# Attention in a fused two-layer kernel: row maxima spread over the partitions by two transfers through memory instead of by TensorE, and the work between the score blocks put in another order

## The chip, the cores and the metric

The kernel runs on one core of one Trainium2 chip, as one launch. Its time is the device time of that launch in microseconds (us). Three runs of the kernel before took 1915.51, 1917.42 and 1915.51 us (median 1915.51). The change is judged against that median.

## The reference

Two layers over `x` of shape (4, 1024, 128). Only the attention of layer 0 is touched by the change:

```python
# layer 0: xn = layernorm(x)
qkv = xn @ W_qkv                       # 128 -> 3 * 64 * 16, 16 heads of 64
scores = einsum('bqhd,bkhd->bhqk', q, k) / 8
weights = softmax(scores)              # row maximum, exp, sum, division
s = einsum('bhqk,bkhd->bqhd', weights, v).reshape(b, s, 1024) @ W_out
x = x + s * silu(experts(xn) + shared_expert(xn))   # 8 experts, top 2
# layer 1: a recurrence over time and a gated MLP with 4-bit weights and inputs
```

W_qkv is large (scaled by 8), so scores are large and the row maximum has to be taken off before the exponential.

## The kernel before, in words

The program has stages in a row: norm and router, attention (`layer0_attention`), expert tiles, layer 1. Attention takes the stretch from about 75 to 1507 us of the span.

Attention works on pairs of heads: 4 batches times 8 pairs are N = 32 pairs, and one pair of heads is 16 steps. In step `t` the scores of 128 keys (`kt = t % 8`) against 512 queries (`hf = t // 8`, the half) are computed for both heads at once: a block of 128 partitions (keys) by 2 x 512 columns (queries). Keys lie on the partitions, so the maximum over keys for each query can't be read off this block. It is found beforehand from a rougher product with queries on the partitions:

- `row_max` on TensorE multiplies q_hi by k_hi (two matmuls of 64 x 128 x 512) into the one PSUM tile `ps_m`; VectorE reduces it (L1546). Eight such steps make a "unit", the maxima of 512 queries; the last reduction (L1549) leaves them in `mxw`, 128 partitions x 2 heads x 4 groups of queries.
- These maxima have to lie along the columns, the same on every partition. Before the change TensorE does this: `max_rows` (L1241) transposes `mxw` by a product with the identity, VectorE multiplies by a mask (`shifts`, L1560) into `shift`, `spread` (L1293) multiplies ones by `shift` into a score bank, and ScalarE copies the result to SBUF (`keep_shift`, L1444, the tile `shift_all`, which is named `qkv_raw` in the trace because it lies over it).
- For each step ScalarE then writes the negated maxima into the score bank (`seed`, L1449), TensorE adds the scores in three products of high and low parts (`scores`, L1286), and ScalarE takes the exponential (L1464) into a ring of eight `probs` tiles.

TensorE multiplies V by `probs` into `ps_v` (`values`, L1301), two steps later. GpSimd adds the `probs` tiles up (L1529), and the denominators come from a product of ones with that sum.

Two steps are a "visit"; a pair has visits 0 to 7. In each visit TensorE does, in this order: `row_max`, `scores`, `scores`, `row_max`, then the first item of the table `VISIT`, then `values` for two steps, then the other items of `VISIT`. Items are: projections of K and Q for the next pair (K0, K1, Q0, Q1, halves of 512 tokens, L1214), rows of V (V0, V1, L1231), denominators (den0, den1, L1250), output projections (out0, out1, L1259), and max0, max1 (L1241). All items share one PSUM bank, `ps_x`, so each waits until the one before it has been read. Of a K or Q projection ScalarE reads the high part (L1412), then VectorE the rest (`low`, L1554).

The two score banks `ps_s` alternate, and `seed` of step t+2 waits for the exponential of step t. The order of every engine is fixed by this hand-written table and by the code; nothing is rearranged at run time. SyncE issues the transfers in program order and stops at each wait. In the trace k_hi, k_lo, q_hi, q_lo of even pairs are called `e_ew`, and den, rden, raw, attn are `e_y_row`, because later tiles lie over them.

Of the kernel before, what the change touches and what calls it, by code (L numbers as in the profile page):

```python
# [75 lines left out]
def layer0_norm_and_router(nc, ctx, g):  # L76
# [61 lines left out]
    with nc.Block() as block:  # L138
        @block.sync
        def _(sp):  # L140
# [24 lines left out]
        def _(pool):  # L165
# [27 lines left out]
        def _(act):  # L193
# [794 lines left out]
def layer0_attention(nc, ctx, g):  # L988
# [9 lines left out]
    EARLY = 3  # L998
# [3 lines left out]
    PRESETS = 5  # L1002
    LATE_PRESETS = 7
# [1493 lines left out]
```

## Time and profile before

| what | value |
|---|---|
| median of 3 runs | 1915.51 us |
| the profiled execution, its device time | 1918.03 us |
| its span in the trace | 1916.2 us |
| time outside the span | 1.8 us |
| granted TensorE clock, whole span | 0.982 |
| attention stage | about 75 to 1507 us, 32 pairs |

All durations below come from the profiled execution, which is 2.5 us above the median of the runs. Its page gives the busy time of each engine: TensorE 93%, VectorE 78%, ScalarE 78%, GpSimd 75% of the span. In the attention stage the engines work beside each other in the same 16-step rhythm, so a share of the whole span does not say which one sets the pace there; that is read from the order in time within one pair, where an engine without idle time before its instructions is the one that the others wait for.

### The profile page before, as it was taken

Reading aid. Unit: us, or ns where it says so; the run is one execution under the profiler, and the core shown is the slowest. Engines: PE = TensorE matmul, PEld = TensorE weight load, DVE = VectorE, ACT = ScalarE, POOL = GpSimd, SP = SyncE. Lnnn points to the kernel's source line nnn. Section 1 sums busy time; section 2 is a strip of 40 time slices with the busy share of each in tenths; the row PEclk is TensorE's granted clock in tenths of the full one; section 3 lists DMA queues with packets and bytes.
Section 4 is the critical chain, followed back from the end, with each engine's and each line's share of the span. In section 5 each row is a group of like instructions: output and inputs, shape, how many; then the busy total and the mean of one; then the engine's idle time right before and its main releaser. Section 6 shows DMA issues by size and latency. Waiting matters only on the chain. (4 is left out here: it accounts for less than half of the span.)

```text
span 1916.2 us, 32241 instructions
## 1 busy us (share of the span) xinstructions
PE 1776.4 (93%) x9630; PEld 958.1 (50%) x9630; DVE 1486.4 (78%) x2052; ACT 1485.6 (78%) x2017; POOL 1434.9 (75%) x870
## 2 busy tenths in 40 slices
PE   5799999999999999999999999999999899985688
PEld 4444444444444444444444444444444488863456
DVE  6777777777777777777777777777777698888896
ACT  4488888888888888888888888888888688874553
POOL 4388888888888888888888888888888456765663
PEclk9999999999999999999999999999999999997898
DMA  7101010101011010101010101011010477531000
GB/s 248 46 13 55 11 56 15 59 11 55 22 44 42 25 55 11 55 11 55 12 55 19 55 20 46 22 44 56 11 55 11 153 230 247 158 99 50 1 17 28
DMA packets 98438, 108.95 MB, mean 57 GB/s; under 512 B 8161, under 2 KB 88097, under 8 KB 95202
## 3 DMA queue, kind: packets, MB, share of 16 engines
q1 hardware_dynamic: 93410, 98.26, 16.1%
q0 software_dynamic: 4992, 10.27, 1.6%
q8 instruction: 16, 0.26, 0.1%
q14 instruction: 20, 0.16, 0.0%
HBM read 53.12 MB, written 27.38 MB: 42 GB/s over the span
## 5 line engine op out<-in xcount | busy, mean ns | idle before, releaser
L1529 POOL TENSOR_TENSOR psum_k<-psum_k,probs 128x1024 f32<-128x1024 f32 x384 | 926.4, 2412 | 183.7 <-ACT probs L1464 168.6
L1546 DVE TENSOR_REDUCE mxh<-ps_m 128x2 f32<-128x1024 f32 x518 | 628.4, 1213 | 276.1 <-PE ps_m L1273 275.7
L1464 ACT ACTIVATE probs<-ps_s 128x1024 f32<-128x1024 f32 x512 | 496.4, 1022 | 132.4 <-PE ps_s L1286 93.2
L1301 PE MATMUL ps_v<-probs,V 128*64 128x512 f32 x2056 | 489.8, 597 | 0.0
L1449 ACT ACTIVATE ps_s<-qkv_raw 128x1024 f32<-128x1024 f32 x449 | 445.9, 1030 | 7.1
L1570 DVE RECIPROCAL e_y_row<-e_y_row 128x128 f32<-128x128 f32 x256 | 241.8, 945 | 30.2 <-ACT e_y_row L1420 21.1
L1301 PEld LDWEIGHTS ps_v<-probs,V 128*64 128x64 f32 x2056 | 137.6, 137 | 224.9 <-issue 188.4
L1529 POOL TENSOR_TENSOR psum_k<-probs 128x1024 f32<-128x1024 f32 x64 | 152.4, 2381 | 65.7 <-ACT probs L1464 57.9
L1286 PE MATMUL ps_s<-e_ew 64*128 64x512 f32 x1536 | 198.9, 390 | 1.1 <-ACT qkv_raw L1444 1.0
L1286 PEld LDWEIGHTS ps_s<-e_ew 64*128 64x128 f32 x1536 | 145.9, 184 | 28.6 <-ACT qkv_raw L1444 1.4
L859 POOL DMA_INDIRECT results<-e_y_row,e_y_at x92 | 103.7, 1128 | 67.4 <-ACT e_y_row L800 45.2
L1273 PE MATMUL ps_m<-e_ew 64*128 64x512 f32 x524 | 131.5, 498 | 11.4 <-DVE mxh L1546 10.2
L1273 PE MATMUL ps_m<-k_hi,q_hi 64*128 64x512 f32 x512 | 128.0, 496 | 4.0 <-DVE mxh L1546 3.6
L1273 PEld LDWEIGHTS ps_m<-e_ew 64*128 64x128 f32 x524 | 49.1, 184 | 114.8 <-DVE mxh L1546 68.2
L1286 PE MATMUL ps_s<-q_hi,k_lo 64*128 64x512 f32 x512 | 101.6, 391 | 0.0
L1286 PE MATMUL ps_s<-q_hi,k_hi 64*128 64x512 f32 x512 | 101.5, 391 | 0.0
L1286 PE MATMUL ps_s<-q_lo,k_hi 64*128 64x512 f32 x512 | 101.2, 389 | 0.0
L1273 PEld LDWEIGHTS ps_m<-k_hi,q_hi 64*128 64x128 f32 x512 | 47.6, 183 | 106.5 <-DVE mxh L1546 60.1
L784 ACT ACTIVATE e_relu<-e_ps_z 128x512 f32<-128x512 f32 x124 | 74.2, 598 | 26.5 <-PE e_ps_z L713 25.6
L905 DVE TENSOR_TENSOR e_h_lo<-e_relu,e_h_hi 128x512 fp32r<-128x512 f32 x124 | 87.5, 711 | 1.2 <-ACT e_h_hi L789 1.2
L901 DVE TENSOR_TENSOR e_relu<-e_relu 128x512 f32<-128x512 f32 x108 | 74.5, 690 | 15.5 <-ACT e_relu L784 15.2
L789 ACT ACTIVATE e_h_hi<-e_relu 128x512 fp32r<-128x512 f32 x124 | 78.2, 631 | 6.0 <-DVE e_relu L901 5.9
(322 smaller groups left out, 2938.1 us busy)
## 6 DMA issues: line engine op xcount, KB each, us to landing
e_ew<-w_split SPq DMA_DIRECT2D x23, 1024.0 KB
V<-e_x_raw SPq DMA_DIRECT2D x33, 512.0 KB, 3.6
xs_hi<-xh SPq DMA_DIRECT2D x16, 512.0 KB, 4.1
xs_lo<-xl SPq DMA_DIRECT2D x16, 512.0 KB, 4.7
rows<-in_blank_d SPq DMA_DIRECT2D x4, 1483.5 KB, 16.2
e_x_raw<-rows SPq DMA_DIRECT2D x23, 258.0 KB, 3.0
we_raw<-in_experts_d SPq DMA_DIRECT2D x33, 128.0 KB, 2.5
w_split<-we_hi SPq DMA_DIRECT2D x32, 128.0 KB, 1.9
```

The source lines that it names most:

```text
L789: nc.scalar.activation(h_hi[:, q % NH, :], r2[:, q % NH, :], ACT.Copy).then_inc(hi_done, 1)
L859: nc.gpsimd.indirect_dma_start(g.results[:, :], bass.IndirectOffsetOnAxis(ap=y_at[s][:, t, 0:1], axis=0), y_row[s][:, t, :], None).then_in ...
L901: nc.vector.tensor_tensor(r2[:, q % NH, :], r[:, q % NZ, :], r[:, q % NZ, :], ALU.mult).then_inc(sq_done, 1)
L905: nc.vector.tensor_tensor(h_lo[:, q % NH, :], r2[:, q % NH, :], h_hi[:, q % NH, :].bitcast(F32), ALU.subtract).then_inc(lo_done, 1)
L1273: ins = nc.tensor.matmul(m[:, x, :], q_hi[par][rows, q:q + P], k_hi[par][rows, kh * CH:(kh + 1) * CH], start=True, stop=True)
L1286: ins = nc.tensor.matmul(o[:, x, :], lhs[par][rows, keys], rhs[par][rows, qs], start=False, stop=True, skip_group_check=True)
L1301: ins = nc.tensor.matmul(ps_v[rows, :], V[par][:, kt, rows], probs[:, t % RING, x, :], start=kt == 0, stop=kt == KT - 1)
L1449: nc.scalar.activation(ps_s[t % 2][:, :, :], shift_all[:, :, :], ACT.Copy).then_inc(seeded, 1)
L1464: nc.scalar.activation(probs[:, t % RING, :, :], ps_s[t % 2][:, :, :], ACT.Exp, scale=SCALE).then_inc(p_done, 1)
L1529: nc.gpsimd.tensor_tensor(acc, probs[:, (t - 1) % RING, :, :] if kt == 1 else acc, probs[:, t % RING, :, :], ALU.add).then_inc(add_done, 1)
L1546: nc.vector.tensor_reduce(mxh[:, kh, t, :], max_bank(unit, i)[:, :, :], AX.X, ALU.max).then_inc(m_done, 1)
L1570: ins = nc.vector.reciprocal(rden[:, cols], den[:, cols])
```

## The change

TensorE no longer turns and spreads the maxima. The last reduction of a unit writes `mx` (128 x 2 x 4). SyncE waits for it and writes its 1024 values to memory (`peaks`, each 4 bytes at its own place), waits until they have landed, and reads them back into all 128 partitions (`peak[hf]`, 128 x 1024, 512 KB). Every seed, the first of a half too, is a copy of `peak[hf]` times -1; those of steps 3 and 15 (`BY_V`) are made by VectorE, the other 14 of a pair by ScalarE. The maxima run one more step ahead of the scores (`EARLY` 4 instead of 3).

The items stand in another order: at most one item stands before `values`, and den1, den0 are the last of their visits. K0 of a pair is computed in visit 7 of the pair two before it, not in visit 0 of the one before it. ScalarE's rounding of the next weights (`w_hi`) moves from visit 7 to visit 5, GpSimd's (`w_lo`) from the end of the pair to step 11, and the expert part from visit 4 to visit 0.

```diff
-    EARLY = 3
+    EARLY = 4
-    VISIT = [("out0", "K0"), ("den1", "Q0"), ("max1", "V0"), ("K1",), ("out1",), ("den0", "Q1"), ("max0", "V1"), ()]
-    LATE = ("K1", "out1")
+    VISIT = [("out0",), ("Q0", "den1"), ("V0",), ("K1",), ("Q1", "den0"), ("V1",), ("out1",), ("K0",)]
-    FIRST = ["K0", "Q0", "K1", "Q1", "V0", "V1", "V2", "max0", "V3"]
+    FIRST = ["K0", "Q0", "K1", "Q1", "V0", "V1", "V2", "V3", "K0+"]
+    BY_V = (3, 15)
...
+            def spread(unit, hf):          # on SyncE
+                sp.wait_ge(mx_done, unit + 1)
+                sp.dma_start(g.peaks[hf:hf + 1, :].rearrange("a (x t q) -> q (a x) t", x=2, t=4), mx[:, :, :],
+                             allow_slow_non_contiguous=True).then_inc(mx_out, 16)
+                sp.wait_ge(mx_out, unit * 16 + 16)
+                sp.dma_start(peak[hf][:, :, :].rearrange("p x c -> p (x c)"), g.peaks[hf:hf + 1, :].to_broadcast([P, 2 * CH])).then_inc(peak_in, 16)
             load_part(0)
+            spread(0, 0)
...
                 sp.dma_start(xs_lo[:, :].bitcast(F32), g.xl[:, batch].bitcast(F32)).then_inc(xs_in, 16)
+                spread(n * 2 + 1, 1)
                 expert_part(n)
                 load_part(n + 1)
+                spread(n * 2 + 2, 0)
+                spread(n * 2 + 3, 1)
                 expert_part(n + 1)
                 load_part((n + 2) % N)
+                spread(n * 2 + 4, 0)
                 sp.wait_ge(xa_done, reads(n + 1, "V1"))
                 move(0)
...
                     scores(n, par, t)
                     row_max(n * 2 + unit, i, other, unit % 2)
-                    if t % KT == KT - 1:
-                        pe.wait_ge(shift_done, n * 2 + t // KT + 2)
-                        pe.wait_ge(p_done, P0 + n * STEPS + t)
-                        spread(1 - t // KT, 0).then_inc(spread_ready, 1)
                     for name in VISIT[p][:1]:
-                        if name not in LATE:
-                            item(n, par, name, b)
+                        item(n, par, name, b)
...
-            def keep_shift(k):
-                act.wait_ge(spread_ready, k)
-                nc.scalar.activation(shift_all[:, :, :], ps_s[0][:, :, :], ACT.Copy).then_inc(seeded, 1)
+            def seed(n, t):                # on ScalarE
+                hf = t // KT % 2
+                if t % KT < 2:
+                    act.wait_ge(peak_in, peaks_of(n, t))
+                act.wait_ge(p_done, P0 + n * STEPS + t - 1)
+                nc.scalar.activation(ps_s[t % 2][:, :, :], peak[hf][:, :, :], ACT.Copy, scale=-1.0).then_inc(seeded, 1)
...
+            def seed(n, t):                # on VectorE, steps 3 and 15
+                v.wait_ge(p_done, P0 + n * STEPS + t - 1)
+                v.wait_ge(peak_in, peaks_of(n, t))
+                nc.vector.tensor_scalar(ps_s[t % 2][:, :, :], peak[t // KT][:, :, :], -1.0, None, ALU.mult).then_inc(seeded_v, 1)
...
-                shifts(n, "max1")
...
+                add_out(n, "out1")
+                seed(n, 15)
                 step(14)
```

TensorE, the end of visit 3 of an even pair, before (rows from the second `row_max`, named L1273, to the next visit's first; `shift1` holds the maxima of the second half):

```order
L1273 MATMUL ps_m<-k_hi1,q_hi1 128x512 x2
L1373 REGISTER_ALU
L1293 MATMUL ps_s0<-shift1,ones_r 128x512 x2
L1301 MATMUL ps_v<-probs,V0 64x512 x4
L1214 ISA
L1214 MATMUL ps_x<-xh,w_hi 128x512
L1215 REGISTER_ALU
L1215 MATMUL ps_x<-xl,w_hi 128x512
L1216 MATMUL ps_x<-xh,w_lo 128x512
L1270 REGISTER_ALU
L1273 MATMUL ps_m<-k_hi1,q_hi1 128x512 x2
```

The same place now (L1286 is `row_max` here, L1233 to L1235 the projection K1, L1311 `values`):

```order
L1286 MATMUL ps_m<-k_hi1,q_hi1 128x512 x2
L1233 ISA
L1233 MATMUL ps_x<-xh,w_hi 128x512
L1234 REGISTER_ALU
L1234 MATMUL ps_x<-xl,w_hi 128x512
L1235 MATMUL ps_x<-xh,w_lo 128x512
L1309 REGISTER_ALU
L1311 MATMUL ps_v<-probs,V0 64x512 x2
L1309 REGISTER_ALU
L1311 MATMUL ps_v<-probs,V0 64x512 x2
L1283 REGISTER_ALU
L1286 MATMUL ps_m<-k_hi1,q_hi1 128x512 x2
```

The spreading product L1293 is gone, and K1 stands ahead of `values` instead of behind it.

ScalarE at the same boundary, before (L1464 exponentials, L1444 the kept copy, L1449 the seed, L1412 the read of K1):

```order
L1464 ACTIVATE probs<-ps_s0 128x1024
L1464 ACTIVATE probs<-ps_s1 128x1024
L1444 ACTIVATE qkv_raw<-ps_s0 128x1024
L1449 ACTIVATE ps_s1<-qkv_raw 128x1024
L1412 ACTIVATE k_hi1<-ps_x 128x512
L1464 ACTIVATE probs<-ps_s0 128x1024
```

Now (L1472 exponentials, L1419 the read of K1, L1456 the seeds):

```order
L1472 ACTIVATE probs<-ps_s0 128x1024
L1472 ACTIVATE probs<-ps_s1 128x1024
L1419 ACTIVATE k_hi1<-ps_x 128x512
L1456 ACTIVATE ps_s0<-peak1 128x1024
L1456 ACTIVATE ps_s1<-peak1 128x1024
L1472 ACTIVATE probs<-ps_s0 128x1024
```

The read of K1 stands between the exponentials and the seeds, and the first seed of the half comes from `peak1`, which a transfer fills.

SyncE now, in an even pair (L1153 moves V, L1169 writes the maxima, L1172 reads them back):

```order
L1153 DMA V<-e_x_raw 128x8x128
L1183 ISA
L1183 DMA xs_hi<-xh 128x1024
L1184 REGISTER_ALU
L1184 DMA xs_lo<-xl 128x1024
L1168 REGISTER_ALU
L1169 DMA peaks<-mx 128x8x1
L1171 ISA
L1172 DMA peak<-peaks 128x1024
```

Before, the transfers of the expert part followed directly on `xs_lo`.

## Rows read from the trace of the kernel before

**Rows 1.** The page, its head and part 1.
```profile
span 1916.2 us, 32241 instructions
PE 1776.4 (93%) x9630; PEld 958.1 (50%) x9630; DVE 1486.4 (78%) x2052; ACT 1485.6 (78%) x2017; POOL 1434.9 (75%) x870
```

**Rows 2.** Instructions of line 1444, one per half pair: durations, first and last start.
```profile
L1444 ACT ACTIVATE qkv_raw<-ps_s x65: 1023/1032/1032, 75.2 to 1507.4; 128x1024 f32<-128x1024 f32 x65
```

**Rows 3.** Windows, visits 1, 4, 5, 7, then all eight: PE, PEld, DVE, ACT, POOL, clock.
```profile
753.81:759.92 6.11, 5.94 (x32) 2.71 (x32) 4.00 (x4) 5.00 (x6) 5.43 (x4) 1.00 0.03 11
...
771.13:776.10 4.97, 4.97 (x30) 2.23 (x29) 3.55 (x4) 4.25 (x5) 3.39 (x2) 1.00 0.00 0
776.10:782.26 6.16, 5.94 (x33) 2.68 (x32) 5.19 (x5) 5.37 (x8) 5.29 (x4) 1.00 0.03 11
...
787.89:792.58 4.69, 4.62 (x27) 2.12 (x26) 4.11 (x5) 3.86 (x5) 3.92 (x2) 1.00 0.40 112
sum 44.74, PE 43.52 PEld 20.85 DVE 34.02 ACT 37.30 POOL 36.97; mean PE 5.44 PEld 2.61 DVE 4.25 ACT 4.66 POOL 4.62
```

**Rows 4.** Timeline of TensorE in that pair: start, length, line, [idle before <- releaser].
```profile
755.62 0.50 PE L1273 MATMUL ps_m<-k_hi,q_hi 64*128 64x512 f32 x2
756.30 1.08 PE L1250 MATMUL ps_x<-psum_k,ones 128*64 128x512 f32 x4 [0.17 <-DVE e_ew L1554]
...
761.74 0.50 PE L1273 MATMUL ps_m<-e_ew 64*128 64x512 f32 x2
762.56 0.44 PE L1241 MATMUL ps_x<-ident,mxw 128*64 128x128 f32 x4 [0.32 <-DVE e_ew L1554]
762.83 1.89 PE L1301 MATMUL ps_v<-probs,V 128*64 128x512 f32 x8
...
767.37 0.50 PE L1273 MATMUL ps_m<-e_ew 64*128 64x512 f32 x2
767.94 0.49 PE L1293 MATMUL ps_s<-shift,ones_r 64*128 64x512 f32 x2
768.37 1.94 PE L1301 MATMUL ps_v<-probs,V 128*64 128x512 f32 x8
...
772.95 0.49 PE L1273 MATMUL ps_m<-e_ew 64*128 64x512 f32 x2
773.37 1.94 PE L1301 MATMUL ps_v<-probs,V 128*64 128x512 f32 x8
...
778.21 0.50 PE L1273 MATMUL ps_m<-e_ew 64*128 64x512 f32 x2 [0.22 <-DVE mxh L1546]
```

**Rows 5.** Timeline of ScalarE in visit 1 of that pair.
```profile
755.12 1.94 ACT L1464 ACTIVATE probs<-ps_s 128x1024 f32<-128x1024 f32 x2 [0.61 <-PE ps_s L1286]
757.42 0.60 ACT L1420 ACTIVATE e_y_row<-ps_x 128x512 f32<-128x512 f32 x1 [0.36 <-PE ps_x L1250]
757.91 1.97 ACT L1449 ACTIVATE ps_s<-qkv_raw 128x1024 f32<-128x1024 f32 x2
```

**Rows 6.** The page, part 5: group, busy, mean ns, idle before.
```profile
L1546 DVE TENSOR_REDUCE mxh<-ps_m 128x2 f32<-128x1024 f32 x518 | 628.4, 1213 | 276.1 <-PE ps_m L1273 275.7
```

**Rows 7.** The page, part 6: issues, KB each, median us to landing.
```profile
V<-e_x_raw SPq DMA_DIRECT2D x33, 512.0 KB, 3.6
xs_lo<-xl SPq DMA_DIRECT2D x16, 512.0 KB, 4.7
w_split<-we_hi SPq DMA_DIRECT2D x32, 128.0 KB, 1.9
```

**Rows 8.** DMA view, 1519.8 to 1520.7 us: queue, packets, MB, engines' share.
```profile
q1 hardware_dynamic: 244, 0.00, 12.3%
```

**Rows 9.** Timeline, visit 0 of the even pair that begins at 703.03: SyncE.
```profile
709.67 1.07 SPq L1171 DMA_DIRECT2D xs_lo<-xl  x1
```

**Rows 10.** Timeline, the start of attention: last reduction of the first unit, first exponentials.
```profile
68.12 0.17 DVE L1549 TENSOR_REDUCE mxw<-mxh 128x8 f32<-128x16 f32 x1
...
77.43 1.98 ACT L1464 ACTIVATE probs<-ps_s 128x1024 f32<-128x1024 f32 x2
```

More of the change, by code:

```diff
@@ L1121, in rounded, with seeds_before, peaks_of @@
         upto = sum(k[0] in "KQ" for k in names[:names.index(name) + 1])
-        return upto if n is None else n * 4 + 4 + upto
+        return upto if n is None else n * 4 + 5 + upto
+    def seeds_before(t):
+        return t - sum(k < t for k in BY_V)
+    def peaks_of(n, t):
+        return n * 32 + (t // KT + 1) * 16
     def added(t):
@@ L1234, in v_rows @@
                 ins.then_inc(x_ready, 1)
-            def max_rows(n, name):
-                bank_free(n, name)
-                pe.wait_ge(mx_done, 1 if n is None else n * 2 + (2 if name == "max1" else 3))
-                for x, rows in enumerate(HEADS):
-                    ins = nc.tensor.matmul(bank(n, name)[rows, 0:P], mxw[:, x, :], g.ident[:, :], start=True, stop=True)
-                ins.then_inc(x_ready, 1)
             def denominators(n, name):
@@ L1288, in scores @@
                 ins.then_inc(s_ready, 1)
-            def spread(hf, k):
-                for x, rows in enumerate(HEADS):
-                    ins = nc.tensor.matmul(ps_s[k][:, x, :], ones_r[rows, :], shift[hf][rows, :], start=True, stop=True)
-                return ins
             def values(n, par, t, seen):
@@ L1339, in _ @@
             first_max(0, 4, 5, 6, 7)
-            first("V0", "V1", "V2", "max0")
+            first("V0", "V1", "V2", "V3")
             pe.wait_ge(hi_done, rounded(None, "Q1"))
             first_max(1, *range(EARLY))
-            first("V3")
+            pe.wait_ge(n_read, 1)
+            pe.wait_ge(m_done, KT + EARLY)
+            for k in range(2):
+                for x, rows in enumerate(HEADS):
+                    ins = nc.tensor.matmul(ps_s[k][:, x, :], k_hi[0][rows, 0:P], q_hi[0][rows, 0:CH], start=True, stop=True)
+            ins.then_inc(armed, 1)
+            first("K0+")
             pe.wait_ge(preset, LATE_PRESETS)
+            pe.wait_ge(xa_done, AHEAD["a"])
             pe.wait_ge(xv_done, AHEAD["v"])
-            pe.wait_ge(n_read, 1)
             for x, rows in enumerate(HEADS):
                 nc.tensor.matmul(ps_v[rows, :], ones[:, :], probs[:, 0, x, :], start=True, stop=False)
-            pe.wait_ge(shift_done, 1)
-            pe.wait_ge(m_done, KT + EARLY - 1)
-            spread(0, 1)
-            spread(0, 0).then_inc(spread_ready, 1)
             for n, par in pairs(pe):
-                b = (n + 1) // PAIRS % B
                 for t in range(STEPS):
                     p = t // 2
+                    b = (n + (2 if p == VISITS - 1 else 1)) // PAIRS % B
                     unit, i = maximum(t)
@@ L1689, in _ @@
                 add_out(n, "out0")
+                seed(n, 3)
                 step(2)
-                low(n, "K0", nxt)
                 step(3)
+                low(n, "Q0", nxt)
+                expert_part(n)
+                step(4)
                 inverse(n, 1, 0)
-                step(4)
-                low(n, "Q0", nxt)
                 step(5)
-                shifts(n, "max1")
                 inverse(n, 1, 1)
@@ L2450, in layouts @@
     blank[:, D] = 2 * NT + np.arange(ROUTED * CH)
-    mask = np.zeros((2, DH, 4), np.float32)
-    for j in range(4):
-        mask[:, j, j] = -1.0
     return {
```

153 lines of the change are left out of this document (73 added, 80 removed).

## The prediction, as it was put on record before the change was run

> **What bounds the kernel now.** I read the page first: TensorE is busy 93% of the span, VectorE, ScalarE and GpSimd 75 to 78% [rows 1]. That makes TensorE the suspect and nothing more. Line 1444 runs once per half pair, 65 times from 75.2 to 1507.4 us [rows 2], so a pair takes 2 x 1432.2 / 64 = 44.76 us, and attention is 32 of them, 1432 of 1916 us. Next come the windows, one per visit, of the pair that begins at 747.84: the eight add up to 44.74 us, in which TensorE is busy 43.52, ScalarE 37.30, GpSimd 36.97, VectorE 34.02, at a granted clock of 1.00 [rows 3]. Since the ends of matmuls are modelled, I then looked at starts in the timeline: nearly every TensorE instruction follows the one before it at a fixed distance, and the exceptions are few [rows 4]. ScalarE's exponentials wait for TensorE [rows 5], and VectorE's reductions waited 275.7 us for `ps_m` over the kernel [rows 6]. So TensorE sets the pace, and a pair is worth what is taken out of its row.
>
> **What goes out of TensorE's row.** A plain distance from the second `row_max` to what follows is 772.95 to 773.37, 0.42 us. Against it, per pair:
> - Spreading product: 767.37 to 768.37 is 1.00 us with L1293 between, so it costs 0.58, twice: 1.16.
> - max0 and max1: 761.74 to 762.83 is 1.09 us, so 0.67 each, of which 0.40 is the wait for VectorE's `low` (the bank must be read). Twice: 1.34.
> - den1 behind the second `row_max` waits for `low` of K0: 755.62 to 756.30, 0.68 instead of 0.42: 0.26 in visit 1. Now den1 stands behind Q0 and `values`.
> - Visit 5: the second `row_max` comes 778.21 - 776.10 = 2.11 us after the first, against 755.62 - 753.81 = 1.81 in visit 1, since out1's addition stands before the reduction on VectorE: 0.30. In the new table out1 is one of the items before `values`, done earlier.
>
> All from [rows 3, 4]. Sum 3.06 us a pair; 44.74 - 3.06 = 41.68. K0 only moves. In the new order a visit with one item should last 4.96 (visit 4 now: 4.97), and visits 1 and 4 with two items 5.86 (visit 5 now: 6.16 - 0.30) [rows 3]: 6 x 4.97 + 2 x 5.86 = 41.5, nearly the same.
>
> **Do the other engines keep up with 41.7?** ScalarE loses two of 16 copies of about 0.98 us (two take 1.97 [rows 5]): 37.30 - 1.97 = 35.3 busy. VectorE loses two products of 512 columns and gains two seeds of 1024 columns. The trace has no such instruction with SBUF in and PSUM out; the nearest is the reduction of 1024 columns out of PSUM, 1.21 us [rows 6]; below, it could be half of that, above, I allow 1.4. I take 1.2; VectorE then has about 35. GpSimd does the same 36.97. None reaches 41.7, but a visit can still be too long for one. The tightest is visit 6, with two reductions, a reciprocal, out1's addition and the seed of step 15. Visit 5 now has the same with the expert difference in the seed's place, 5.19 us busy [rows 3], against a visit of 4.97: about 0.1 to 0.3 late, caught up in visit 7. ScalarE reads the item between the exponentials and the seeds: exponentials begin 1.31 into a visit (755.12 - 753.81), are through 1.82 later, the projection ends about 3.2 into it, its read is followed by the seed after 0.49 (757.42 to 757.91), so seeds start at about 3.7 and the first is done at 4.7 [rows 5]; the next visit's scores begin at 4.97 + 0.33. Half a microsecond of slack. I put 0.10 us a pair for new small waits, with 0 and 0.6 as ends.
>
> **The transfers.** They leave no instruction on TensorE, but the first seeds of a half wait for them, and behind these on ScalarE stand all later ones. The last `row_max` of a unit is the second of visit 1 or 5: 1.81 + 0.50 + 1.21 + 0.17 [rows 3, 4, 6, 10], about 3.8 us into it (4.0 in visit 5, where a reciprocal stands before). The seeds that need it are due 3.7 into visit 3 or 7, and may be 0.5 late. That is free time of 5.86 + 4.97 + 3.7 - 3.8 + 0.5 = 11.2 us for the second half and 2 x 4.97 + 3.7 - 4.0 + 0.5 = 10.1 us for the first.
> What they take: the read back is 512 KB to 128 partitions like the move of V, 3.6 us; behind other traffic 4.7 [rows 7]. The write is 1024 pieces of 4 bytes, 64 for each of 16 DMA engines, and the trace has none like it. From below: a store of 128 pieces of 1 KB lands in 1.9 us; the move of V, also 1024 pieces though of 512 bytes, in 3.6 [rows 7]. On the rate of 4-byte pieces I found one stretch: 244 packets in 0.9 us, with the engines 12.3% busy [rows 8], so 0.123 x 16 x 900 / 244 = 7 ns of engine time each, but only one in 59 ns per engine (16 x 900 / 244). If 59 ns is the pace at which they are made, 64 need 3.8 us beside the 1.9: 5.7. I take 4.6, between 3.6 and 5.7, nearer neither; as an upper end 8 us, if a write to memory of 4 bytes costs twice such a read. The chain is 4.6 + 3.6 + 0.3 for SyncE's two waits = 8.5 us, with ends of 7.5 and about 12. Under 10.1 it costs nothing.
> In even pairs the write stands in the same queue behind `xs_lo`, issued 709.67 - 703.03 = 6.64 into visit 0 and landed 4.7 later, at 11.3 [rows 7, 9]; the maxima are ready at 4.97 + 3.8 = 8.8. So the chain begins up to 2.5 us late there, in the half that has 11.2: 8.5 + 1.0 to 2.5 is 9.5 to 11.0. Just free.
> On SyncE the blocking waits stand before the expert part, whose stores and loads have whole visits of time, and before the move of V, which is needed only in the next pair's visit 1, over 15 us later.
> The Trainium skill, "DMA: Bandwidth & Descriptors", section "Rules for kernel authors", says that a non-contiguous last dimension lowers to one descriptor per element, and its "Specifications" that under 512 bytes the DMA engine reads, modifies and writes. The first agrees with the 1024 pieces that I count; of the second no row of this trace shows a price for stores, and it speaks for the upper end above.
>
> **Start and end.** Before, 9.31 us lie between the first unit's maxima and the first exponentials (68.12 to 77.43) [rows 10]. Now the chain of 8.5, a seed of 1.0 and about 1.1 for scores give 10.6 or more: +2 us with the extra step and K0+. The end is unchanged.
>
> **Sum.** 32 x (3.06 - 0.10) - 2 = 93 us. The profiled execution took 1918.03 (span 1916.2 and 1.8 around it): 1825. It stands 2.5 above the median of the runs, so 1915.5 - 93 = 1822.5; I say 1822.
>
> **The rivals.**
> - A, the forecast: TensorE stays the pace, the chain is covered. 44.74 - 41.5 = 3.2 a pair and no start cost gives 1813; 0.6 of new waits and some more at the start 1838. Own range 1812 to 1842. Chance 0.72.
> - B, the chain is late in part: 10.1 to 12.2 us. At 11.2 the first half of each pair is 1.1 us late, the even pairs' second half about 1.5 (queueing), so 32 x 1.1 + 16 x 1.5 = 59 us given back: 1881; milder cases down to 1840. For it: 59 ns a piece and the queue behind `xs_lo`; against: 3.6 us for as many pieces of V. Chance 0.12.
> - C, slower: the store of 4-byte pieces is so slow that the seed of the first step of each half waits for it. Every us above 10.1 and 11.2 stops ScalarE and then TensorE; from (c - 10.1) + (c - 11.2) = 3.0, c = 12.2, nothing is gained, a bit sooner with the queue. At c = 14 it is 3.9 + 2.8 - 3.0 = 3.7 us a pair: 1915.5 + 118 = 2034. It needs a store of about 8.3 us or more, or a read back that is slowed since all partitions ask for the same 4 KB. Against it: 7 ns of engine time a piece. Chance 0.09. The read-modify-write rule of the Trainium skill named above would work in this direction.
> - D, VectorE or ScalarE takes over in visits 6 and 7 (a seed of 1.4, a read between exponentials and seeds that comes too late): 1 us a pair, 32 us: 1854. For it: 5.19 against 4.97; against: whole-pair sums of 35 against 41.7. Chance 0.07.
>
> **How the numbers follow.** The median of three runs can tell 0.2% (4 us) from nothing. A, D and most of B are faster: 0.72 + 0.07 + 0.09; within 0.2%: 0.02, from B; slower: C and the rest of B, 0.10. The range takes A, D and half of B: 1810 to 1870, 0.85.
>
> **What would show it.** Right: pairs of 41.6 to 42 us; no matmul between the second `row_max` and the item; the second `row_max` 1.81 after the first in every visit; ScalarE's seeds of steps 0, 1, 8, 9 issued at once behind the item's read; the maxima's write landing in 4 to 6 us, the read back in 3.6 to 4. Wrong: idle time of ScalarE before those seeds, released by the read back (B, C); distances of 2.1 and more between the two `row_max` of visit 7 (D); a store above 8 us. A TensorE clock below 1.00 in the stretch would be something I have not reckoned with.

## The result, and the profile after

The changed kernel takes 2200.75 us (median of 4 runs, 2195.82 to 2212.92); beside them the kernel before took 1916.47 us (1915.51 to 1919.24). The ratio is 1.149, with a 95% interval of 1.144 to 1.154: slower by 15%. The forecast was 1822 us with a range up to 1870, and the sign was wrong too.

The head of the page after and its part 1, against [rows 1]:

```profile
span 2195.8 us, 32039 instructions
PE 1860.2 (85%) x9247; PEld 996.3 (45%) x9247; DVE 1519.2 (69%) x2053; ACT 1433.5 (65%) x1954; POOL 1438.9 (66%) x868
```

Every engine's share has fallen, TensorE's from 93 to 85% and ScalarE's from 78 to 65%. No engine took over, so all of them wait for something else. Part 5 (busy, mean ns | idle before, releaser) and part 6 (KB each, us to landing) name it; the V row answers to that of [rows 7]:

```profile
L1456 ACT ACTIVATE ps_s<-qkv_raw 128x1024 f32<-128x1024 f32 x224 | 221.7, 1021 | 141.2 <-DMA qkv_raw<-peaks 141.2
L1456 ACT ACTIVATE ps_s<-peak 128x1024 f32<-128x1024 f32 x224 | 222.2, 1023 | 129.5 <-DMA peak<-peaks 129.5
...
qkv_raw<-peaks SPq DMA_DIRECT2D x33, 512.0 KB, 4.2
V<-e_x_raw SPq DMA_DIRECT2D x33, 512.0 KB, 5.1
peak<-peaks SPq DMA_DIRECT2D x32, 512.0 KB, 4.4
```

ScalarE's seeds wait 270.7 us for the read back of the maxima, in 64 halves: 4.23 us each. The read back itself lands in 4.2 to 4.4 us (3.6 reckoned). The rest is the store, seen in SyncE's timeline (start, length, line) and in its row of the waits (in all, times, longest):

```profile
807.40 0.39 SPq L1169 DMA_DIRECT2D peaks<-mx  x1
817.71 0.32 SPq L1172 DMA_DIRECT2D qkv_raw<-peaks  x1
...
SPq L1172 <- DMA peaks<-mx: 610.3, 64, 11.6
```

From the store's issue to the read back's issue 10.3 us pass here and 10.0 in the mean of all halves; SyncE waits 9.5 of them for the store, where 4.6 were forecast. The same boundary on ScalarE and on TensorE:

```profile
814.68 1.94 ACT L1472 ACTIVATE probs<-ps_s 128x1024 f32<-128x1024 f32 x2 [2.11 <-PE ps_s L1302]
816.67 0.60 ACT L1419 ACTIVATE k_hi<-ps_x 128x512 fp32r<-128x512 f32 x1
822.07 1.97 ACT L1456 ACTIVATE ps_s<-qkv_raw 128x1024 f32<-128x1024 f32 x2 [4.80 <-DMA qkv_raw<-peaks]
```

```profile
818.43 0.50 PE L1286 MATMUL ps_m<-e_ew 64*128 64x512 f32 x2
823.15 2.71 PE L1302 MATMUL ps_s<-e_ew 64*128 64x512 f32 x12 [4.22 <-ACT ps_s L1456]
825.66 0.63 PE L1286 MATMUL ps_m<-e_ew 64*128 64x512 f32 x2
```

The seeds could have begun at 817.27 (822.07 - 4.80). They begin 14.7 us after the store's issue, so the free time was 9.9 us and the chain 14.7, against 10.1 and 8.5 forecast. This is a first half; of the second half that follows, the store on SyncE and the seeds on ScalarE:

```profile
833.15 0.38 SPq L1169 DMA_DIRECT2D peaks<-mx  x1
```

```profile
848.39 1.97 ACT L1456 ACTIVATE ps_s<-peak 128x1024 f32<-128x1024 f32 x2 [4.41 <-DMA peak<-peaks]
```

Here 10.8 us were free (11.2 forecast) and the chain took 15.2. And the scores behind the first of these stalls last 2.71 us where they last 1.55 elsewhere. The windows (length, busy of PE, PEld, DVE, ACT, POOL, granted clock, DMA share, GB/s) say why:

```profile
819.00:823.00 4.00, 0.00 (x0) 0.00 (x0) 1.32 (x2) 0.93 (x1) 2.97 (x4) 1.00 0.84 244
823.00:826.00 3.00, 2.85 (x14) 1.92 (x14) 0.00 (x0) 2.39 (x5) 0.00 (x0) 0.57 0.00 1
826.00:829.00 3.00, 3.00 (x14) 0.85 (x12) 2.35 (x3) 1.85 (x2) 1.99 (x1) 0.86 0.00 0
829.00:832.00 3.00, 3.00 (x20) 1.89 (x19) 2.32 (x3) 2.34 (x4) 1.60 (x3) 1.00 0.46 127
...
829.24:835.11 5.87, 5.87 (x34) 2.68 (x32) 4.39 (x6) 5.29 (x7) 4.39 (x4) 1.00 0.78 260
835.11:840.13 5.02, 5.02 (x32) 2.67 (x30) 4.01 (x4) 4.16 (x6) 4.01 (x3) 1.00 0.15 24
```

TensorE stands still for 4 us, and in the 3 us behind that its granted clock is 0.57, near the lower of its two levels (1.2 instead of 2.4 GHz). The last two rows are visits away from the stall, against [rows 3]: 5.87 and 5.02 us, where 5.86 and 4.96 were forecast. Between the stalls the new order does what it was reckoned to do.

A pair lasts 53.23 us: the 512 exponentials start between 83.8 and 1783.9, so 16 steps take 16 x 1700.1 / 511.

### The profile page after: what moved, and what is told of

Same layout as the page of the kernel before. It is cut to its first block and busy times, and to the rows that moved or that the text cites. A ratio compares the mean times of both kernels' runs of the same rounds, so it can differ in the third digit from the quotient of the medians.

```text
span 2195.8 us, 32039 instructions
## 1 busy us (share of the span) xinstructions
PE 1860.2 (85%) x9247; PEld 996.3 (45%) x9247; DVE 1519.2 (69%) x2053; ACT 1433.5 (65%) x1954; POOL 1438.9 (66%) x868
## 5 line engine op out<-in xcount | busy, mean ns | idle before, releaser
L1472 ACT ACTIVATE probs<-ps_s 128x1024 f32<-128x1024 f32 x512 | 503.6, 1023 | 189.6 <-PE ps_s L1302 188.9
L1311 PE MATMUL ps_v<-probs,V 128*64 128x512 f32 x2056 | 505.9, 613 | 0.0
L1302 PE MATMUL ps_s<-e_ew 64*128 64x512 f32 x1536 | 236.8, 445 | 125.9 <-ACT ps_s L1456 123.6
L1456 ACT ACTIVATE ps_s<-qkv_raw 128x1024 f32<-128x1024 f32 x224 | 221.7, 1021 | 141.2 <-DMA qkv_raw<-peaks 141.2
L1456 ACT ACTIVATE ps_s<-peak 128x1024 f32<-128x1024 f32 x224 | 222.2, 1023 | 129.5 <-DMA peak<-peaks 129.5
L1311 PEld LDWEIGHTS ps_v<-probs,V 128*64 128x64 f32 x2056 | 136.1, 143 | 268.3 <-issue 246.6
L1302 PEld LDWEIGHTS ps_s<-e_ew 64*128 64x128 f32 x1536 | 159.6, 210 | 170.9 <-ACT ps_s L1456 138.1
L1302 PE MATMUL ps_s<-q_hi,k_hi 64*128 64x512 f32 x512 | 121.0, 467 | 104.9 <-ACT ps_s L1456 104.9
L1286 PE MATMUL ps_m<-e_ew 64*128 64x512 f32 x524 | 135.6, 514 | 7.0 <-DVE mxh L1550 6.3
L1286 PE MATMUL ps_m<-k_hi,q_hi 64*128 64x512 f32 x512 | 132.0, 512 | 0.0
L1286 PEld LDWEIGHTS ps_m<-e_ew 64*128 64x128 f32 x524 | 53.7, 202 | 152.5 <-issue 108.1
L1286 PEld LDWEIGHTS ps_m<-k_hi,q_hi 64*128 64x128 f32 x512 | 52.3, 201 | 141.9 <-issue 103.8
L1302 PE MATMUL ps_s<-q_lo,k_hi 64*128 64x512 f32 x512 | 116.0, 445 | 0.0
L1302 PE MATMUL ps_s<-q_hi,k_lo 64*128 64x512 f32 x512 | 116.0, 446 | 0.0
L1302 PEld LDWEIGHTS ps_s<-q_hi,k_hi 64*128 64x128 f32 x512 | 55.8, 214 | 122.8 <-ACT ps_s L1456 116.0
L1272 PE MATMUL ps_x<-e_y_row,wo 128*64 128x512 f32 x260 | 91.2, 788 | 0.8 <-issue 0.8
```

What stands on the lines that cost most here:

```text
L1272: ins = nc.tensor.matmul(ps_x[rows, :], wo[1 - par][:, rows], attn[:, :], start=True, stop=True)
L1286: ins = nc.tensor.matmul(m[:, x, :], q_hi[par][rows, q:q + P], k_hi[par][rows, kh * CH:(kh + 1) * CH], start=True, stop=True)
L1302: ins = nc.tensor.matmul(o[:, x, :], lhs[par][rows, keys], rhs[par][rows, qs], start=False, stop=True, skip_group_check=True)
L1311: ins = nc.tensor.matmul(ps_v[rows, :], V[par][:, kt, rows], probs[:, t % RING, x, :], start=kt == 0, stop=kt == KT - 1)
L1456: nc.scalar.activation(ps_s[t % 2][:, :, :], peak[hf][:, :, :], ACT.Copy, scale=-1.0).then_inc(seeded, 1)
L1472: nc.scalar.activation(probs[:, t % RING, :, :], ps_s[t % 2][:, :, :], ACT.Exp, scale=SCALE).then_inc(p_done, 1)
```

## The experiments

The names in the diffs are those of the changed kernel unless said otherwise. Kernels of one group ran beside each other, each with runs of the kernel before: 1916.6 us in the first group, 1925.5 in the second, 1925.7 in the third.

**Smaller cost of the store, no transfers at all, and a real alternative.** First, pieces of 32 bytes:

```diff
-sp.dma_start(g.peaks[hf:hf + 1, :].rearrange("a (x t q) -> q (a x) t", x=2, t=4), mx[:, :, :], ...
+sp.dma_start(g.peaks[hf:hf + 1, :].rearrange("a (q x t) -> q (a x) t", x=2, t=4), mx[:, :, :], ...
```

> The changed kernel with one difference in place: each partition writes its 8 maxima side by side (32 bytes, 128 pieces) instead of at 1024 places of 4 bytes. The maxima then come back in another order, so the values are wrong, and the exponential has a scale of 1/8000 instead of 1/8 so that all stays finite; the work is the same. Theory T1, the store of 4-byte pieces is the whole miss: the wait for the store falls from about 10 us to about 2 to 2.5, the read back stays at 4.3, the chain is 6.5 to 7.5 and under the 9.9 that are free; ScalarE's waits for the read back (270.7 us in the changed kernel) go to under 10, the granted clock goes back to 1.00, and the time is 1815 to 1835. Theory T2, the read back and the queueing matter as much as the store (the 512 KB read from one 4 KB row, transfers ahead in the queue): the waits fall only by half, 1950 to 2050. Theory T3, the new order itself runs slower than reckoned: above 1850 although ScalarE waits for no transfer.

Measured: 1839.01 us, ratio 0.959 (0.958 to 0.961). SyncE waits 86.4 us over 65 times for the store, 1.3 each, and no seed waits for a transfer. Second, the store and the read back happen once, ahead of the loop:

```diff
 with sp.Fori(0, N // 2) as i:
-    spread(n * 2 + 1, 1)
-    spread(n * 2 + 2, 0)
...
```

> The changed kernel with the two transfers done only once, at the start; all seeds of all pairs use the first unit's maxima, so no seed in the loop waits for a transfer, and 64 writes and read backs are gone. The values are wrong, with the exponential's scale at 1/8000 so that all stays finite. T1 and T2: this is the ceiling of the new order, pairs of 41.7 us, 1815 to 1830. T3: above 1850. The difference to the run with packed writes is what the transfers cost beside the stall (contention, clock): T1 says under 10 us.

Measured: 1840.51 us (0.960, 0.959 to 0.962), the same as with 32-byte pieces. So transfers that are in time cost nothing, and some 1838 us, not 1822, is what the new order is worth. Both times lie above the ranges of T1 (up to 1835 and 1830) and below the 1850 of T3: T1 has the cause, but its ranges were built around the prediction's 1822, which leaves out small waits and a later start (see below). Third, VectorE turns the maxima in blocks of 32x32, and four stores write 8 rows of 128 bytes each:

```diff
+nc.vector.transpose(mxT[:, :], mx[:, :]).then_inc(mx_done, 1)
...
+for k in range(4):
+    q = slice(k * 32, (k + 1) * 32)
+    sp.dma_start(g.peaks[hf:hf + 1, :].rearrange("a (c q) -> (a c) q", c=8)[:, q], mxT[k * 32:k * 32 + 8, :]).then_inc(mx_out, 16)
```

> The changed kernel, all values right, but VectorE turns the 128 x 8 maxima in blocks of 32 x 32 first, and SyncE writes them with four transfers of 8 rows of 128 bytes each (32 pieces in all) instead of 1024 pieces of 4 bytes. T1: four issues of about 0.4 us and 2 us to land, so 3.5 to 4 us for the store, chain 8 to 8.5 us with the turn, under 9.9 for the first half and under 11.2 for the second but for even pairs behind xs_lo, where it is near the edge: 1815 to 1850. T2: 1900 and more. T3: above 1850 without waits for a transfer.

Measured: 1837.27 us, 0.959 (0.958 to 0.961). It beats both kernels. SyncE's timeline, and the windows of visits 0, 1, 3 of the pair from 714.30 and the sum of its eight:

```profile
723.50 1.34 SPq L1173 DMA_DIRECT2D peaks<-mxT  x4
725.71 0.34 SPq L1176 DMA_DIRECT2D peak<-peaks  x1
```

```profile
714.30:719.42 5.12, 5.03 (x30) 2.19 (x28) 4.51 (x5) 3.79 (x5) 4.79 (x6) 1.00 0.00 0
719.42:725.30 5.88, 5.88 (x34) 2.69 (x33) 4.42 (x7) 5.30 (x7) 5.41 (x4) 1.00 0.04 12
...
730.43:735.45 5.02, 5.02 (x29) 2.39 (x27) 3.85 (x4) 4.40 (x6) 4.66 (x3) 1.00 0.00 0
...
sum 42.25, PE 42.09 PEld 19.90 DVE 35.88 ACT 35.14 POOL 37.30; mean PE 5.26 PEld 2.49 DVE 4.48 ACT 4.39 POOL 4.66
```

Four stores take 2.2 us together, TensorE is busy 42.09 of 42.25 us, and the chain is 2.2 + 3.9 to 4.1 + 0.2 = 6.3 to 6.5 us under a free time of 10. Behind `xs_lo`, in the second half of even pairs, the four stores take 3.3 us in the mean, still in time.

**Which stores are slow?** Small stores to memory were added to the kernel before, on SyncE's queue where it is idle, one behind the other, 16 times over the kernel, whose time they leave at 1920 to 1929 us. Their form is

```diff
+def probe(n, k, dst, src):
+    sp.dma_start(dst, src, allow_slow_non_contiguous=True).then_inc(pr_sem, 16)
+    sp.wait_ge(pr_sem, n * 64 + (k + 1) * 16)
```

> The kernel before, with six small transfers once per two pairs on SyncE's queue, one after the other with nothing else in flight, and nobody waiting for their data. Kernel time about that of before (1916, up to +5). Prices, T1: 1024 stores of 4 bytes as in the change 9 to 10 us; 128 stores of 32 bytes 2 us; 512 stores of 4 bytes 5 to 6; 8 rows of 512 bytes 2; 1024 stores of 4 bytes that lie 64 bytes apart: 9 to 10 if the number of pieces is the price, much less if it is that neighbouring pieces share a line of memory; 1024 loads of 4 bytes: 4 to 6 if writing to memory is the dear part, 9 to 10 if the pace of pieces is. T2: the 1024 stores take under 6 us when nothing is ahead of them in the queue.

> The kernel before with eight small stores to memory per two pairs, one behind the other, on a queue that is idle there, each with a wait for its completion: first 1,024 pieces of 4 bytes, 64 bytes apart; second 8 rows of 512 bytes; third 1,024 pieces of 4 bytes side by side (the changed kernel's); fourth 128 pieces of 4 bytes side by side; fifth 128 pieces 64 bytes apart; sixth 1,024 pieces 512 bytes apart; seventh 1,024 pieces 32 bytes apart; eighth the 8 rows again. Theory line (pieces in the same 64 bytes wait for each other): the third and the fourth take 8 to 9 us, the first, fifth and sixth 2.2 to 3 us, the seventh (two to 64 bytes) in between or like the first. Theory small write (any write to memory of 4 bytes is slow, for it has to be read, merged and written): all but the second and the eighth take 6 to 9 us. Theory count: the first, third, sixth and seventh take 8 us, the fourth and fifth 2 to 3 us; the 512 pieces that took as long as 1,024 speak against it already.

> The kernel before with small stores one behind the other on the idle queue: 128 pieces of 4 bytes at a spacing of 32, 16, 8 and 4 bytes (2, 4, 8 and 16 of them in the same 64 bytes), then 16 pieces of 4 bytes side by side (one stretch of 64 bytes), 128 pieces of 8 bytes side by side (8 to 64 bytes), 128 of 16 bytes (4 to 64 bytes), and 8 rows of 512 bytes. Theory turns (each further piece in the same 64 bytes costs some 0.4 us): 2.9, 3.7, 5.3 and 8.4 us; the 16 pieces 8.4 as well; 8 bytes 5.3, 16 bytes 3.7. Rival threshold (only full chains of 4-byte neighbours are slow, or pieces below some size): the first three 2.5 us, or all of them 8 us; the pieces of 8 and 16 bytes 2.5 us. The kernel with pieces of 16 bytes, whose store took 2.2 us in the mean instead of 3.5 to 4, speaks against the same price for pieces of 16 bytes.

> The kernel before with small stores on the idle queue, all of 4-byte pieces: 16, 32, 64, 128 and 256 side by side, then 32 at a spacing of 8 bytes, 16 at a spacing of 64 bytes, and 8 rows of 512 bytes. The run before showed 1.3 us (median) for 16 pieces side by side and 8 us for 128, with the same 16 pieces in each 64 bytes, and 1.4, 1.9, 3.5 and 8.0 us for 128 pieces 32, 16, 8 and 4 bytes apart. Theory chain (a DMA is dealt out to 16 engines in order, so of n pieces each engine has n/16 neighbours, and those that it writes into the same 32 bytes go one behind the other, at about 1 us each): 16, 32, 64, 128, 256 side by side take 1.4, 1.9, 3.5, 8 and 8 us, since the chain is 1, 2, 4, 8 and 8 long; the 32 pieces 8 bytes apart 1.9. Theory place (only the pieces per 64 bytes count, and 16 alone are an exception of one stretch): 32, 64, 128 and 256 all 8 us; the 32 pieces 8 bytes apart 3.5.

One pass of the second of these, in SyncE's timeline (each start less the one before is a store with its wait):

```profile
740.80 0.38 SPq L1167 DMA_DIRECT2D pr_out<-pr  x1
743.40 0.29 SPq L1167 DMA_DIRECT2D pr_out<-pr8r  x1
744.63 0.39 SPq L1167 DMA_DIRECT2D pr_out<-pr  x1
753.15 0.33 SPq L1167 DMA_DIRECT2D pr_out<-pr  x1
761.51 0.33 SPq L1167 DMA_DIRECT2D pr_out<-pr  x1
764.07 0.37 SPq L1167 DMA_DIRECT2D pr_out<-pr  x1
```

1,024 pieces of 4 bytes take 2.60 us when they are 64 bytes apart and 8.52 when they are neighbours; 128 neighbours take 8.36, and 2.56 when apart. Issue to next issue, mean in us over the 16 passes of one run each:

| stores of 4-byte pieces | us |
|---|---|
| 1,024: side by side | 9.4, 9.6 |
| 1,024: 32, 64, 512 bytes apart | 2.8, 2.4, 2.5 |
| 512 side by side | 9.1 |
| 256 side by side | 8.1 |
| 128: side by side | 7.7, 8.0, 8.0 |
| 128: 8, 16, 32, 64 bytes apart | 3.5, 1.9, 1.4, 2.0 |
| 64, 32, 16 side by side | 6.8, 3.1, 1.3 |
| 16 side by side, in the third experiment | 1.8 (1.3 to 3.3) |
| 32, 8 bytes apart | 3.1 |
| 16, 64 bytes apart | 1.3 |
| 128 of 8, 16, 32 bytes, side by side | 3.4, 2.1, 1.6 |
| for comparison, a load of the 1,024 | 2.3 |

"Count" is wrong from 128 upward, and "any 4-byte write" is wrong: what is slow are small pieces next to each other, 32 or more of them. With 128 pieces the price fades at a spacing of 16 bytes; with 32 pieces a spacing of 8 bytes took off nothing (3.1 us both times). My finer theories fell as well. That pieces in the same 64 bytes go one behind the other doesn't hold for 16 alone (1.3 us). The chain per DMA engine gave 1.9 and 3.5 us for 32 and 64 pieces; they took 3.1 and 6.8, and the rise ends at 128 where it should end. The trace doesn't show which engine writes which piece, so the mechanism stays open; the table is what is shown. It isn't the engines' work: in the DMA view of the changed kernel from 807.40 to 817.70, 40 slices (busy tenths), its 1,040 packets are through after six slices of 0.26 us, and what follows is waiting for completion.

```profile
DMA  0002770000000000000000000000000000000000
...
q1 hardware_dynamic: 1040, 0.00, 4.5%
```

The Trainium skill, "DMA: Bandwidth & Descriptors", section "Anatomy of one DMA — SWDGE (gpsimd) path", says that the semaphore's update waits until the last byte has landed, that this can take surprisingly long for a target in HBM, and that it is most of a fixed cost of about 2 us. The trace agrees in the order, packets first and then a wait, for a transfer that SyncE issued. The size roughly holds for pieces 64 bytes apart (2.4 us in all) and not for neighbours (9.4 to 9.6); here the measurement decides.

**Inside the kernel.** To the alternative (1837 us) a second store of the same maxima was added ahead of the read back, once as 1,024 neighbours, once 64 bytes apart:

```diff
+sp.dma_start(g.probe[0:1, 0:1024 * s].rearrange("a (c q s) -> q (a c) s", c=8, s=s)[:, :, 0:1], mx[:, 0:8].unsqueeze(2), ...)  # s = 1 or 16
+sp.wait_ge(mx_out, unit * 80 + 80)
```

> The kernel that turns the maxima on VectorE (1837 us), with one more store between its own store and the read back: the maxima once more as 1,024 pieces of 4 bytes side by side in memory, into a buffer that nobody reads. Theory line (16 pieces in the same 64 bytes of memory wait for each other, some 0.4 us each): the trace of the small stores on an idle queue gives 8.4 to 8.5 us, the changed kernel itself 9.5 to 10.3; the chain becomes 2.2 + 9.5 to 10.3 + 4.3 = 16 to 17 us against 10 free, 6 to 7 late, and with what follows a stall 2270 to 2340 us. Theory count or traffic (the loss came from the number of pieces, or from other causes of the changed kernel): it and its pair with pieces 64 bytes apart come out alike.

> The same with the pieces 64 bytes apart: as many pieces of 4 bytes, from the same partitions, and only the places in memory differ. Theory line: the small store takes 2.4 to 3.3 us, the chain 9 to 10 us, at the edge of the free time: 1838 to 1865 us. Theory count: as its pair, 2270 us or more.

Measured: 2335.56 us (ratio 1.212, 1.209 to 1.215) and 1843.55 us (0.959, 0.956 to 0.961). The two kernels issue the same instructions and move the same bytes; 492 us hang on the distance of the pieces in memory. Both times lie within the forecasts of theory line, and not alike, as theory count had it. SyncE's wait for this store, first in the one with neighbours, then in the other:

```profile
SPq L1179 <- DMA probe<-mx: 594.0, 64, 10.5
```

```profile
SPq L1179 <- DMA probe<-mx: 134.9, 65, 2.6
```

**Half of the pieces.**

```diff
-sp.dma_start(g.peaks[hf:hf + 1, :].rearrange(... x=2, t=4), mx[:, :, :], ...
+sp.dma_start(g.peaks[hf:hf + 1, 0:CH].rearrange(... x=1, t=4), mx[:, 0:1, :], ...
-sp.dma_start(peak[hf][:, :, :]..., g.peaks[hf:hf + 1, :].to_broadcast([P, 2 * CH]))
+sp.dma_start(peak[hf][:, :, :], g.peaks[hf:hf + 1, 0:CH].unsqueeze(1).to_broadcast([P, 2, CH]))
```

> The changed kernel with half of the pieces: only the maxima of the first head are stored (512 pieces of 4 bytes, neighbours in memory, where there were 1,024), and the read back spreads these 512 numbers to both heads, still 512 KB. The second head is shifted by the first head's maxima, and the exponentials' scale is 1/8000, so the values differ and the work is the same. Theory count (the store's time is so many pieces at so much each): the store falls from 9.5 us to about 5, the chain from 14.7 to 10, no wait is left, 1840 to 1870 us. Theory line (what takes long is that neighbouring four-byte pieces fall into the same stretch of memory, 16 to every 64 bytes, whatever their number): in the experiment with small transfers on an idle queue 512 such pieces took as long as 1,024 (8.3 to 8.8 us), so the store stays at 9 to 10 us and the kernel at 2170 to 2200 us.

Measured: 2299.43 us (1.192, 1.190 to 1.195), outside both forecasts. SyncE's wait for the store stays (587.7 us over 64 halves, 9.2 each), which speaks against "count". The surplus is my edit's: the read back, now twice the same 2 KB per partition, lands in 6.7 us instead of 4.2.

**What lateness costs, and the clock.** Small loads in a row between store and read back of the alternative, with no 4-byte piece in it:

```diff
+for k in range(DELAY + 1):
+    sp.wait_ge(mx_out, unit * TURN + 64 + k * 16)
+    if k < DELAY:
+        sp.dma_start(late[0:8, :], g.peaks[hf:hf + 1, :].rearrange("a (c q) -> (a c) q", c=8)).then_inc(mx_out, 16)
```

> The same with one small load between the store and the read back: chain 9.1 us of 10 free. Theory lateness: nothing is late, 1837 us as without it, within 0.3%. Rival (the free time is smaller than reckoned, or part of the visits' 0.57 us per pair is a share of these waits): 1845 us or more.

> The kernel that turns the maxima on VectorE and stores them in pieces of 128 bytes (1837 us), with three small loads (8 rows of 512 bytes each), one behind the other, put between the store and the read back. No piece of 4 bytes is in it. By the trace of that kernel the chain is 2.2 us of store, 4.3 of read back and 0.3 of rest, 6.8 us in a free time of 10; each small load should add 2.2 to 2.5 us. Theory lateness (all of the loss is that the maxima are behind): chain 13.6 us, 3.6 us late, and with the lower clock 1.2 to 1.5 us more, 4.8 to 5.1 us x 64 = 310 to 325 us, 2145 to 2165 us. Rival (the pieces of 4 bytes themselves hold up other transfers or engines): well under 2100 us.

Measured: 1841.54 us with one (0.957, 0.955 to 0.960; as without it) and 1865.55 with three (0.969, 0.967 to 0.971). A small load takes 1.3 to 1.5 us here, not the 2.2 to 2.5 that I expected, so the dose was smaller. The 1865.55 us miss the 2145 to 2165 of theory lateness and fall where the rival was to be seen, but the chain was hardly late, so this pair doesn't decide between the two: no run has 4 us of lateness without 4-byte pieces in it. In the kernel with three:

```profile
731.46 1.29 SPq L1176 DMA_DIRECT2D peaks<-mxT  x4
733.63 3.20 SPq L1181 DMA_DIRECT2D late<-peaks  x3
738.02 0.34 SPq L1182 DMA_DIRECT2D peak<-peaks  x1
```

6.6 us to the read back and 4.0 for it make 10.6, and its seeds wait 32.1 us in all, 0.50 per half. So the free time is about 10.1, as reckoned. Then matmuls that nobody needs, in the stall:

```diff
 row_max(n * 2 + unit, i, other, unit % 2)
+if t % KT == 0:
+    pe.wait_ge(xv_done, ...)
+    for k in range(14):
+        nc.tensor.matmul(ps_x[:, :], k_hi[par][:, 0:P], q_hi[par][:, 0:CH], start=True, stop=True)
 scores(n, par, t)
```

> The changed kernel with 14 more matmuls (128x128 by 128x512, about 0.23 us each, 3.2 us together) on TensorE before the first score block of each half, into the item bank that has been read: where TensorE stood still for 4.2 us it now works, and nothing of what it waits for comes earlier. It measures what the lower granted clock after each stall costs. Theory clock (about 1.4 us of the 5.66 us per stall is slower matmuls after it: the granted clock was 0.57 in the 3 us behind the stall, and score blocks took 2.71 us there for 1.55): the clock's mean goes from 0.90 to 0.98 or more, 64 x 1.2 to 1.5 = 75 to 95 us come back, 2105 to 2130 us. Rival (the slow blocks behind the stall wait for something else, such as operands or ScalarE, and the clock only goes with it): 2190 to 2220 us.

Measured: 2163.79 us, 1.123 (1.120 to 1.126) against 1.149 without them: 50 us back for 896 matmuls more. TensorE around one boundary, and the windows behind it:

```profile
780.46 3.49 PE L1381 MATMUL ps_x<-q_hi,k_hi 128*128 128x512 f32 x14
784.79 0.50 PE L1303 MATMUL ps_s<-q_hi,k_hi 64*128 64x512 f32 x2 [0.84 <-ACT ps_s L1461]
...
785.00:788.00 3.00, 3.00 (x19) 1.63 (x19) 1.03 (x1) 2.76 (x4) 0.11 (x1) 1.00 0.00 0
```

The clock stays at 1.00, and its mean over the span is 0.976 for 0.904. I expected 75 to 95 us back and 2105 to 2130 us, so the time lies between the two forecasts; the store took 10.4 us in this kernel instead of 9.5, and the seeds' waits grew from 270.7 to 337.6 us. Why the store got slower no run shows. Per half in us, each span against that of an undisturbed kernel of its group (1835.4, 1838.1, 1840.9):

| kernel | seeds' wait | longer by | difference |
|---|---|---|---|
| changed | 4.23 | 5.63 | 1.40 |
| half of the pieces | 5.88 | 7.26 | 1.38 |
| second store, neighbours | 6.19 | 7.79 | 1.60 |
| matmuls in the stall | 5.28 | 5.03 | -0.25 |
| three small loads | 0.50 | 0.37 | -0.13 |

1.4 to 1.6 us beyond the wait where TensorE stood still for 4 us and more, nothing where it was kept busy or the stall was short: the lower clock is shown to be that part. The rest of the lengthening is the seeds' wait itself; with wait and clock taken off, some 0.2 us per half at most stay open.

**A version without an added instruction.** Partition p takes queries 4p to 4p+3, so its maxima are neighbours and the store has 256 pieces of 16 bytes:

```diff
-q = hf * CH + t * P
+q = slice(hf * CH + t, (hf + 1) * CH, 4)
-g.peaks[hf:hf + 1, :].rearrange("a (x t q) -> q (a x) t", x=2, t=4)
+g.peaks[hf:hf + 1, :].rearrange("a (x q t) -> q (a x) t", x=2, t=4)
```

> The changed kernel with two edits: the row maxima's stationary operand takes every fourth query (4p+t for partition p), so that the four maxima of a partition and head are neighbours in memory, and the store writes 256 pieces of 16 bytes in the order that the read back needs. Nothing is added on any engine. Theory line: four pieces to 64 bytes give 2.4 us and three further turns of some 0.4, 3.5 to 4 us; the chain is 8 to 8.5 us of 10 free, no wait for the transfers is left, 1837 to 1845 us. Rival (any store of pieces under 32 bytes is slow): store 8 us or more, 2100 us or more. Second rival (a stationary operand with a stride loads slower on TensorE): 32 loads per pair, visible as longer weight loads; at 0.1 us each 3 us per pair, 1940 us.

Measured: 1896.89 us, 0.985 (0.983 to 0.987). The store is quick: SyncE waits 119.7 us over 65 times, 1.8 each, less than either theory (3.5 to 4 and 8). The second rival is what happened. TensorE's weight loads of `row_max` (minimum, median, maximum in ns), here and in the alternative:

```profile
L1286 PEld LDWEIGHTS ps_m<-k_hi,q_hi x512: 304/305/306, 91.7 to 1444.2; 64*128 64x128 f32 x171
```

```profile
L1290 PEld LDWEIGHTS ps_m<-k_hi,q_hi x512: 182/183/183, 93.1 to 1395.6; 64*128 64x128 f32 x171
```

0.12 us more for each load. Pairs last 43.7 us instead of 42.1 (starts of the exponentials: 81.4 to 1477.9 against 82.7 to 1428.0). That is 1.6 us. In the timeline what follows a `row_max` starts 0.12 to 0.13 us later than in the alternative (0.47 us after its start for 0.34, 0.55 for 0.43), so one of its two loads shows and the other is hidden; 16 x 0.12 = 2.0, and a part of that falls into waits that were there before. The Trainium skill, "SBUF — State Buffer", section "Door 1: The DMA port swizzle", says that SBUF has lines of 16 bytes and that each access that crosses to a new line pays. With a stride of four 4-byte elements each access is in a new line, so the 305 ns for 183 agree. It also gives 4 fp32 as how far one can stride for free; a stride of four was not free here. Other strides were not tried.

## Why the prediction was wrong

- **The step that failed: the store.** "I take 4.6, between 3.6 and 5.7 ... as an upper end 8 us". It takes 9.5 us of waiting in the mean, 10.0 from issue to issue, and so the chain of 8.5 us, "Under 10.1 it costs nothing", became one of 14.7. I built the price from the rate at which an engine handles packets, and from stores of whole rows. The rate was misread too: 59 ns a piece and engine came from a stretch of small loads of the kernel before [rows 8]; here 1,040 packets, 65 to an engine if they are dealt out evenly, go through in three slices of 0.26 us, at most 12 ns each. The engines are through after about 1.5 us of the ten. What counts is the completion of neighbouring small writes, which no row before showed. The read-modify-write rule of the Trainium skill ("DMA: Bandwidth & Descriptors", "Specifications"), which I named for an upper end and for the rival with 0.09, doesn't tell the cases apart: 1,024 pieces of 4 bytes 64 bytes apart and 128 of 16 bytes are under its 512 bytes as well and take 2.4 and 2.1 us.
- **Rival C was right** in place and condition: "It needs a store of about 8.3 us or more". Its price was too low. At a chain of 14.7 its formula gives (14.7 - 10.1) + (14.7 - 11.2) - 3.0 = 5.1 us a pair, 1915.5 + 163 = 2079; measured 2201. The lateness in it, 8.1 us a pair, is near the 2 x 4.23 that the seeds wait; the difference of 122 is mainly the next three points.
- **The clock.** Named as not reckoned with: 1.4 us x 64 = 90 us.
- **Small waits.** A pair without stalls lasts 42.1 to 42.25 us, not 41.68, since visits 0, 2, 6 and 7 last 5.08 to 5.13 us and visits 3 and 5 5.02 to 5.04, for 4.96 reckoned (starts of the visits in the alternative). That is 0.4 to 0.6 x 32 = 13 to 18 us, for 0.10 a pair in the sum. Part of it is rival D's mechanism at a small price: in visit 0 of the alternative the second `row_max` starts 1.97 us after the first (714.30), for 1.82 elsewhere, since the reduction that it waits for begins on VectorE only at 715.00, behind other work of 1.31 us:

```profile
716.27 0.19 PEld L1290 LDWEIGHTS ps_m<-k_hi,q_hi 64*128 64x128 f32 x2 [0.52 <-DVE mxh L1554]
```

- **The start.** The first exponentials start at 82.71 in the alternative, where no transfer is waited for, against 77.43 [rows 10]: 5.3 us for 2; which of the items moved there makes up the rest was not tried. The own range of forecast A ended at 1842, which held both points, and its centre was 16 too low.
- **Right:** what leaves TensorE's row, as the visits of 5.87 and 5.02 show (of the 3.06 us, 2.5 to 2.7 are left after the small waits); VectorE's seed takes 1.22 us (1.2 taken); the read back 4.2 to 4.4 (3.6 alone, 4.7 behind traffic); the free time 9.9 and 10.8 (10.1 and 11.2). The queue behind `xs_lo`, reckoned at 1.0 to 2.5 us, costs 1.1 in the alternative (3.3 for 2.2). VectorE and ScalarE, busy 35.88 and 35.14 us of a pair, take over nowhere. Rival D, a visit of VectorE's or ScalarE's for 1 us a pair, is out but for the waits named above.

The rise of 284 us between the medians is 279.6 us between the spans of the two profiled executions (1916.2 and 2195.8). Of these 32 x (53.23 - 44.76) = 271 us come in the pairs and 6.4 us at the start (83.8 against 77.43), which leaves 2 us.

## What to carry to other kernels

A store of many pieces smaller than 16 bytes that lie side by side in memory is to be priced by its completion, not by bytes or packets; where a trace has none like it, measure one on an idle queue before putting it on a path. Turn the data on chip, or make the pieces 16 bytes and more, or leave gaps. If a transfer's free time is 10 us, its upper bound should be tested against it first: here an experiment of six small transfers would have turned the forecast. And a stall of TensorE of 4 to 6 us cost its length and a quarter to a third more here.

## What the runs showed of the hardware that I had not expected

- A store of 128 neighbouring 4-byte pieces with its wait takes 7.7 to 8.0 us, of 1,024 of them 9.4 to 9.6; of 1,024 pieces 64 bytes apart 2.4.
- After TensorE stood still for 4 us the granted clock was 0.57 over the next 3 us, and 0.86 over the 3 after; in the kernel with three small loads, whose seeds wait 0.50 us per half, it is 1.00 from 800 to 1400 us.
- A stationary operand with a stride of 16 bytes loads in 305 ns instead of 183.
- A read back in which each partition takes the same 2 KB twice lands in 6.7 us, the same 512 KB from 4 KB in 4.2.
